# Long convolution in 64-step Toeplitz blocks on 64x64 array tiles instead of 128-step blocks on the full array

## The chip, the cores and the metric

The kernel runs on one core of a Trainium2 chip. The metric is the time of one execution in device microseconds (us). A core has TensorE (matmuls, PE in the profile, with its weight loads as PEld), VectorE (DVE), ScalarE (ACT), GpSimd (POOL), SyncE (SP, here only a queue that issues DMAs) and 16 DMA engines. SBUF is the working memory of 128 partitions, PSUM the memory that TensorE writes.

## The reference

One block of a network on `x` of shape (4, 2048, 256), all in float32: a layer norm, then the sum of a gated long convolution and a ternary feed-forward part, added to `x`. Cut to what matters:

```
xn   = layernorm(x)
proj = xn @ in_proj_w + in_proj_b              # 256 -> 768
v    = proj[..., :256]
for i in range(2):                             # the two orders
    ctrl = proj[..., (i+1)*256:(i+2)*256]
    h    = implicit_filter(...)                # (2048, 256): an MLP of time, times exp(-|decay| * t * 2048)
    v    = causal_convolution(v, h)            # along the 2048 steps, a filter of its own for each channel
    xc   = conv3(ctrl) ; v = v * xc * sigmoid(xc @ gate_w + gate_b)
attn = v @ out_proj_w + out_proj_b
r    = relu(bitlinear(xn, w_fc) + gate * low_rank(xn))        # 256 -> 1024
ffn  = bitlinear(r * r, w_proj)                               # 1024 -> 256
out  = x + attn + ffn
```

The filter decays so fast that most of its lags are below the least normal float32. The kernel measures that at run time: it always computes the lags below 257, those from 257 to 384 only for groups of channels in which one filter still has a normal number there, and all the rest only if a flag is set (with these inputs it is not).

## The kernel before, in words

Four stages follow one another, each a block in which the engines run their own programs and meet at semaphores.

**Setup** (`setup_stage`) computes the filters and writes them to `filters` in HBM, one row of 2048 + 127 values for each of 2 x 256 channels, makes the effective feed-forward weights and the flags.

**Projection** (`project_stage`) runs over 16 chunks of 512 tokens, software-pipelined in `step`. For each chunk TensorE makes the control channels `pc` (24 matmuls of 512 columns), then `pn` = V (24 matmuls of 256 columns), then the gates of the chunk before (`gates(0)`, `gates(1)`, 24 of 512), and between them the transposes of the next chunk (`pT`, 8) and of the first gate (`pn`, 8). A product of two float32 operands is made here of three matmuls in the type fp32r, high by high, high by low and low by high (`split_mm`), for which ScalarE makes `xn_hi` as a copy and VectorE `xn_lo` as a difference. V is stored as `V[128, 256 channels, 4 batches, 16 blocks]`: time step within a block of 128 on the partitions.

**Mix** (`mix_stage`) runs over 64 groups of 8 channels (32 groups for each order, GPI = 4 groups to an iteration `it`, 16 iterations), and interleaves the convolution with the feed-forward part of one chunk for each iteration. With blocks of 128 steps the convolution of a channel is a sum over block lags A: output block a gets `T_A` (a 128x128 Toeplitz matrix of the filter) times input block a - A. `conv` issues for each channel and each of A = 0, 1, 2 one plain float32 matmul with `T_A` as the weights and the 4 x (16 - A) block columns of V as the moving side. The Toeplitz matrices are read from `filters` by DMA with overlapping rows (`hankel`): each of the four loads of a group brings two channels of 128 x 384 values into one of four slots of `T`, and waits for the matmuls that read the slot (`tile_mm`). `near(q)` is the pair of channels q. On TensorE a group reads: near(0), the middle block lag if the group's flag is set (`Tmid`, only the pairs whose bit is set), fc(2g), near(1), proj(2g-1), fc(2g+1), near(2), near(3), proj(2g). `fc` is 6 matmuls of 512 columns into `pf`, `proj` 8 matmuls of 256 columns into `pp`, both fp32r. From `pf` the value goes ScalarE relu (`r`), VectorE square, ScalarE `r_hi`, VectorE `r_lo`, and `proj` waits for that (`r_split`). VectorE moves a finished group from `py` to V (`V<-py`), multiplied with GC1 in the first order.

**Output** (`output_stage`) transposes V, multiplies by the second gate, projects and adds, in 16 chunks.

SP's queue issues the loads of `T` and `Tmid` in program order, with a wait before each. POOL's queue issues the chunk loads `xm`, `xb` and stores `xf`. TensorE runs its program in order. What a float32 matmul is on this chip shows in the trace: each plain float32 matmul leaves two LDWEIGHTS and two MATMUL records of the same shape, each fp32r matmul and each transpose one of each.

Of the kernel before, what the change touches and what calls it, by code (L numbers as in the profile page):

```python
# [23 lines left out]
COLS = B * NA  # L24
PADDED = P - 1 + L
NEAR = 3
MID_FROM = (NEAR - 1) * P + 1
FAR_FROM = NEAR * P + 1
FARS = (NA - NEAR - 1) // NEAR
GC = 8  # L30
TC = 2
TILES = GC // TC
# [10 lines left out]
def setup_stage(nc, hbm, ident, bv_row, srow, flag, V, GC1, Win, Wgate, eps, half, load_first, norm):  # L43
    (in_w, in_b, out_b, freqs, w1, b1, w2, b2, w3, b3, decay, gate_w, fast_b, w_fc, w_proj, u, v, gate,
     filters, fc_hi, fc_lo, proj_t) = hbm
    with ExitStack() as ctx:
# [36 lines left out]
        zpad = sb("zpad", [P, 4, P - 1])  # L83
        ones = sb("ones", [P, P])
        win_f = sb("win_f", [P, KT, 3 * D])
# [16 lines left out]
        tile_reach = sb("tile_reach", [1, GROUPS, TILES])  # L102
# [5 lines left out]
        FREQ_LOADS, RANK_LOADS, FILTER_LOADS, PROJ_LOADS, TERN_LOADS = 4, 4, 11, 3, 2  # L108
# [9 lines left out]
        peak_ready, peakT_mm = sem("peak_ready"), sem("peakT_mm")  # L118
# [7 lines left out]
        def _(sp):  # L126
# [27 lines left out]
            load(win_f[:, :, :], in_w.rearrange("(k p) c -> p k c", p=P), proj_in)  # L154
            load(gw_f[:, :, :], gate_w.rearrange("o (k p) c -> p (o k) c", p=P), proj_in)
            load(bv_row[:, :], bass.AP(in_b.tensor, 0, [[0, P], [1, D]]), proj_in)
# [4 lines left out]
            load(rows[:, KT:2 * KT, 0:P - 1], zpad[:, KT:2 * KT, :], stored)  # L161
            for w in range(4):
                sp.wait_ge(h_ready, w + 1)
                at = 0 if w < KT else P - 1
                load(filters[w * P:(w + 1) * P, at:at + L], hT[:, w, :], stored)
# [6 lines left out]
            sp.wait_ge(stored, 16 * 9)  # L172
# [17 lines left out]
        def _(dve):  # L190
# [92 lines left out]
            dve.tensor_copy(srow[:, :], ps[:, 4, 0:D])  # L283
# [3 lines left out]
            link(dve.tensor_reduce(tile_reach[:, :, :], ps[0:1, 5, :].rearrange("p (g q c) -> p g q c", q=TILES, c=TC), AX.X, ALU.max))  # L287
            link(dve.tensor_scalar(reach[:, 0:1], reach[:, 0:1], LEAST_NORMAL, None, ALU.is_ge))
            link(dve.tensor_scalar(tile_reach[:, :, :], tile_reach[:, :, :], LEAST_NORMAL, None, ALU.is_ge))

            groups = reach[:, 1:1 + GROUPS]
            link(dve.tensor_scalar(groups, tile_reach[:, :, TILES - 1], 2.0, None, ALU.mult))
            for q in range(TILES - 2, -1, -1):
                link(dve.tensor_tensor(groups, groups, tile_reach[:, :, q], ALU.add))
                if q:
                    link(dve.tensor_scalar(groups, groups, 2.0, None, ALU.mult))
# [153 lines left out]
def project_stage(nc, x, xnT_hbm, gc2_hbm, ident, bv_row, V, GC1, Win, Wgate, eps, xt, x_loaded, xn_ready, norm, taps, bias_in, gc2_saved):  # L450
    with ExitStack() as ctx:
# [7 lines left out]
        xn = [sb("xn_hi", [P, KT, CH], F32R), sb("xn_lo", [P, KT, CH], F32R)]  # L459
        ctrl = [sb(f"ctrl{i}", [P, 4, CH + 2]) for i in range(2)]  # L460
# [3 lines left out]
        xc = sb("xc", [P, 4, CH])  # L464
        kw, cb, kb, gb = taps[:, :, 0:3], taps[:, :, 3], taps[:, :, 4], taps[:, :, 5]
        pT = ctx.enter_context(nc.psum_tensor("pT", [P, KT, CH], F32))
        pn = ctx.enter_context(nc.psum_tensor("pn", [P, TT, D], F32))
# [4 lines left out]
        xn_hi_done, xn_split = sem("xn_hi_done"), sem("xn_split")  # L472
# [34 lines left out]

        def tapped(buffer, c, k):

            at = 2 - k if c < KT else k  # L510
            return buffer[:, c, at:at + CH]
# [42 lines left out]
        def _(dve):  # L554
# [4 lines left out]
            def step(s, s0):  # L559
# [19 lines left out]
                def tap(c, k_, before, done):  # L579
                    if back:  # L580
                        dve.wait_ge(before, 4 * s - 4 + c + 1)
                        dve.scalar_tensor_tensor(out=xc[:, c, :], in0=tapped(ctrl[1 - par], c, k_), scalar=kw[:, c, k_:k_ + 1],  # L582
                                                 in1=xc[:, c, :], op0=ALU.mult, op1=ALU.add).then_inc(done, 1)

                def low(c):
                    if back:
                        dve.wait_ge(xc_hi_done, 4 * s - 4 + c + 1)
                        dve.tensor_tensor(xcs[c // KT][1][:, c % KT, :], xc[:, c, :], xcs[c // KT][0][:, c % KT, :].bitcast(F32),  # L588
                                          ALU.subtract).then_inc(xc_split, 1)

                def gated(c):
                    dve.wait_ge(gate_done, 4 * s - 4 + c + 1)
                    dve.tensor_tensor(xc[:, c, :], pc[:, c, :], xc[:, c, :], ALU.mult).then_inc(gc_done, 1)
# [19 lines left out]
                if front:  # L613
                    dve.wait_ge(v_mm, s + 1)
                    dve.tensor_tensor(V[:, :, bass.ds(batch(dve, s, s0), 1), TT * k:TT * k + TT].rearrange("p c n a -> p c (n a)"),
                                      pn[:, :, :].rearrange("p i c -> p c i"),
                                      bv_row[:, :].unsqueeze(2).broadcast_to([P, D, TT]), ALU.add).then_inc(v_stored, 1)
# [3 lines left out]
                if ahead:  # L621
                    dve.wait_ge(xn_hi_done, s + 2)
                    if s0 >= 0:
                        dve.wait_ge(xn_saved[1], 16 * s + 16)
                    dve.tensor_tensor(xn[1][:, :, :], pT[:, :, :], xn[0][:, :, :].bitcast(F32), ALU.subtract).then_inc(xn_split, 1)  # L625
# [8 lines left out]
        def _(act):  # L634
# [4 lines left out]
            def step(s, s0):  # L639
# [9 lines left out]
                def first_tap(c):  # L649

                    if back:
                        act.wait_ge(halo_done, 4 * s + c + 1)
                        act.activation(xc[:, c, :], tapped(ctrl[1 - par], c, 0), ACT.Identity, bias=kb[:, c:c + 1],  # L653
                                       scale=kw[:, c, 0:1]).then_inc(tap0_done, 1)

                def high(c):
                    if back:
                        act.wait_ge(xc_ready, 4 * s + c + 1)
                        act.activation(xcs[c // KT][0][:, c % KT, :], xc[:, c, :], ACT.Copy).then_inc(xc_hi_done, 1)
# [661 lines left out]
```

## Time and profile before

| | us |
|---|---|
| median of 3 runs | 1172.76 |
| lowest and highest | 1154.29, 1172.95 |
| the profiled execution, its own time | 1176.48 |
| its span, first to last instruction | 1174.8 |
| mean granted TensorE clock | 0.949 of full speed |

The span and the profiled execution's own time differ by 1.7 us, which lie around the instructions. By stage the span divides into setup 0 to 72, projection 72 to 361, a gap up to 379, mix 379 to 1080, a gap up to 1102, output to the end. In the rows below a time is in us from the span's start unless marked ns; a row of the timeline has start, duration, engine, line, operation, output and inputs and, in brackets, the engine's idle time before it and what ended it. A matmul's duration runs from its start to its modelled end, so that the durations of neighbours overlap; the distance between starts is the pace.

### The profile page before, as it was taken

The numbers are of one execution on the slowest core, as the hardware profiler recorded it, in microseconds if no ns is written. First come the engines' busy times: TensorE is split into PE (matmuls) and PEld (weight loads), VectorE is DVE, ScalarE is ACT, GpSimd is POOL, SyncE is SP. The second block draws the span as 40 slices with busy tenths as digits, with TensorE's granted clock in tenths as the row PEclk, the third lists the DMA queues.
The fourth block names the chain that finished last, engine by engine and source line by source line (L and its number), as shares of the span: only waits on it lengthen the run. The fifth ranks groups of instructions, "written<-read, shape, count | busy, mean of one in ns | idle before, by whom it ended". The sixth has DMA issues, their size and how long they took to land. (4 is left out here: it accounts for less than half of the span.)

```text
span 1174.8 us, 21456 instructions
## 1 busy us (share of the span) xinstructions
PE 1056.6 (90%) x6948; PEld 942.7 (80%) x6949; DVE 624.5 (53%) x1031; ACT 434.6 (37%) x598; POOL 235.2 (20%) x267
## 2 busy tenths in 40 slices
PE   6768999999973999999999999999999999997597
PEld 3357788877863989889898898898898999997586
DVE  7848999999982333333343342342343443343486
ACT  5326777777771222222221122122222222221573
POOL 1044556545601001101101101100101101100011
PEclk9869999999996999989998899998999999999799
DMA  6253323332316888887886897977977877888297
GB/s 168 114 197 127 127 94 138 143 125 92 124 72 218 191 221 191 201 224 147 207 206 158 207 217 192 237 183 164 232 204 176 226 192 189 215 189 266 80 373 266
DMA packets 123605, 214.09 MB, mean 182 GB/s; under 512 B 14212, under 2 KB 101268, under 8 KB 122292
## 3 DMA queue, kind: packets, MB, share of 16 engines
q1 hardware_dynamic: 111572, 168.46, 56.0%
q0 software_dynamic: 11568, 42.08, 9.8%
q10 hardware_dynamic: 432, 3.15, 0.7%
q8 instruction: 17, 0.28, 0.1%
q14 instruction: 16, 0.13, 0.0%
HBM read 164.11 MB, written 49.54 MB: 182 GB/s over the span
## 5 line engine op out<-in xcount | busy, mean ns | idle before, releaser
L999 PEld LDWEIGHTS py<-V,T 128*128 128x128 f32 x3072 | 375.9, 195 | 48.8 <-issue 38.3
L999 PE MATMUL py<-V,T 128*128 x3072 | 373.5, 275 | 30.7 <-DMA T<-filters 30.3
L923 DVE TENSOR_TENSOR r<-r 128x512 f32<-128x512 f32 x128 | 88.6, 692 | 345.3 <-ACT r L951 345.3
L951 ACT ACTIVATE r<-pf 128x512 f32<-128x512 f32 x128 | 76.5, 597 | 461.5 <-PE pf L400 450.4
L925 DVE TENSOR_TENSOR r_lo<-r,r_hi 128x512 fp32r<-128x512 f32 x128 | 92.6, 724 | 89.2 <-ACT r_hi L954 89.2
L984 PE MATMUL pp<-wproj,r_hi 128*128 128x256 f32 x512 | 139.1, 305 | 0.0
L984 PE MATMUL pp<-wproj,r_lo 128*128 128x256 f32 x512 | 129.6, 286 | 0.0
L954 ACT ACTIVATE r_hi<-r 128x512 fp32r<-128x512 f32 x128 | 80.8, 631 | 97.1 <-DVE r L923 97.1
L398 PE MATMUL pf<-xm_hi,wfc_hi 128*128 x256 | 111.9, 437 | 0.7 <-DMA xm_hi<-xnT_hbm 0.5
L582 DVE SCALAR_TENSOR_TENSOR xc<-ctrl,taps,xc 128x512 f32<-128x512 f32 x128 | 99.8, 799 | 17.3 <-ACT xc L653 16.1
L439 POOL TENSOR_SCALAR xt<-xt,norms 128x256 f32<-128x256 f32 x64 | 107.2, 1687 | 3.4 <-POOL norms L433 3.4
L399 PE MATMUL pf<-xm_hi,wfc_lo 128*128 x256 | 103.9, 406 | 0.0
L400 PE MATMUL pf<-xm_lo,wfc_hi 128*128 x256 | 103.8, 406 | 0.0
L984 PEld LDWEIGHTS pp<-wproj,r_lo 128*128 128x128 f32 x512 | 99.9, 195 | 0.0
L984 PEld LDWEIGHTS pp<-wproj,r_hi 128*128 128x128 f32 x512 | 99.3, 194 | 0.0
L872 POOL DMA_DIRECT2D xm_hi<-xnT_hbm x16 | 9.3, 580 | 320.1 <-PE pf L400 250.6
L398 PE MATMUL pc<-xc_hi,wgate_hi 128*128 128x512 f32 x128 | 54.2, 423 | 18.8 <-DVE xc_lo L588 18.8
L879 POOL TENSOR_TENSOR xb<-xb,bo_row 128x1024 f32<-128x1024 f32 x16 | 37.9, 2371 | 148.7 <-DMA xb<-in_attn_x 148.7
L400 PEld LDWEIGHTS pf<-xm_lo,wfc_hi 128*128 128x128 f32 x256 | 50.3, 196 | 12.1
L398 PE MATMUL pc<-xn_hi,win_hi 128*128 128x512 f32 x128 | 53.6, 419 | 4.9 <-DVE xn_lo L625 4.9
L398 PEld LDWEIGHTS pf<-xm_hi,wfc_hi 128*128 128x128 f32 x256 | 50.7, 198 | 7.4 <-issue 1.0
L653 ACT ACTIVATE xc<-ctrl,taps 128x512 f32<-128x512 f32 x64 | 51.9, 810 | 11.1 <-DVE ctrl L576 8.5
(163 smaller groups left out, 1646.6 us busy)
## 6 DMA issues: line engine op xcount, KB each, us to landing
T<-filters SPq DMA_DIRECT2D x256, 384.0 KB, 6.3
xt<-in_attn_x SPq DMA_DIRECT2D x16, 512.0 KB, 4.1
xnT_hbm<-xn_hi SPq DMA_DIRECT2D x16, 512.0 KB, 4.3
xnT_hbm<-xn_lo SPq DMA_DIRECT2D x16, 512.0 KB, 3.8
gc_hbm<-xc SPq DMA_DIRECT2D x16, 512.0 KB, 2.6
xm_hi<-xnT_hbm POOLq DMA_DIRECT2D x16, 512.0 KB, 5.4
xm_lo<-xnT_hbm POOLq DMA_DIRECT2D x16, 512.0 KB, 8.1
xb<-in_attn_x POOLq DMA_DIRECT2D x16, 512.0 KB, 9.6
```

What stands on the lines that cost most here:

```text
L398: pe.matmul(out, w[0], x[0], start=start, stop=False, **more)
L399: pe.matmul(out, w[1], x[0], start=False, stop=False, **more)
L400: return pe.matmul(out, w[0], x[1], start=False, stop=stop, **more)
L439: last = pool.tensor_scalar(buf[:, i, :], buf[:, i, :], mv[:, i, 0:1], rs[:, i:i + 1], ALU.subtract, ALU.mult)
L582: dve.scalar_tensor_tensor(out=xc[:, c, :], in0=tapped(ctrl[1 - par], c, k_), scalar=kw[:, c, k_:k_ + 1], in1=xc[:, c, :], op0=ALU.mult, o ...
L653: act.activation(xc[:, c, :], tapped(ctrl[1 - par], c, 0), ACT.Identity, bias=kb[:, c:c + 1], scale=kw[:, c, 0:1]).then_inc(tap0_done, 1)
L923: dve.tensor_tensor(r[j][:, :], r[j][:, :], r[j][:, :], ALU.mult).then_inc(sq_done, 1)
L925: dve.tensor_tensor(r_lo[j][:, :], r[j][:, :], r_hi[j][:, :].bitcast(F32), ALU.subtract).then_inc(r_split, 1)
L951: act.activation(r[j][:, :], pf[j][:, :], ACT.Relu).then_inc(relu_done, 1)
L954: act.activation(r_hi[j][:, :], r[j][:, :], ACT.Copy).then_inc(r_hi_done, 1)
L984: last = pe.matmul(pp[:, i, :], part[m % 2][:, i * P:(i + 1) * P], wproj[:, m, :], start=(m == 0 and n == 0 and i % 2 == 0), stop=(m == HT ...
L999: last = pe.matmul(y[:, c, :, A:NA], tile[:, j * P:(j + 1) * P], V[:, bass.ds(m * (GPI * GC) + (g * GC + c), 1), :, 0:NA - A] .rearrange(" ...
```

## The change: blocks of 64, four tiles, V as one float32 product

The block is now BW = 64 steps, and a time step within a block takes 64 partitions. The other partition half holds other channels: V is `[128, 128 slots, 4, 32 blocks]`, where a channel lives on partition half `side` and in one of 128 slots. A group is again 8 channels: PAIR = 2 values l, two halves q of the slots, two partition halves `side`. `conv` issues for each l and each A = 0..4 (NEAR is 5) four float32 matmuls with 64x64 weights and 4 x (32 - A) moving columns, one for each pair (side, q): rows of the array by `side`, columns and output partitions by `q`, output bank by `side`. Their moving side is `vwin`, a copy of the group's part of V that ScalarE makes one group ahead. The filters are stored in another order of rows, so that a group's loads are two DMAs of 64 partitions x 4 channels x 320 values, into one of two buffers `T0`, `T1`, which are free when the group two before is done (`group_mm`). The middle lags are now two blocks of 64 (MID = 2) for all 8 channels of a flagged group, loaded into one of two `Tmid`. On TensorE a group reads: conv of l = 0, the middle if flagged, fc(2g), proj(2g-1), fc(2g+1), conv of l = 1, proj(2g).

In the projection, V is one plain float32 product: weights `xnT` (128 x 64 tokens), moving side the 128 columns of one half of the channels, output on partitions 0 to 63 or 64 to 127, 32 matmuls a chunk. For it ScalarE copies `pT` to `xnT` ahead of `xn_hi`, and VectorE takes `xn_lo` from `xnT`. The transposes, the stores of the gates and their loads in the output stage follow the new layout, in the same count of TensorE instructions; the second gate's load is two DMAs of 64 partitions. Setup stores the filters in more DMAs (the second order's rows by halves), stores the 256 scales to HBM, from where the mix stage reads them back, and has a shorter chain of flag instructions.

The core of the diff ("..." marks what is left out):

```diff
-NEAR = 3
+BW = 64
+SIDES = P // BW
+SLOTS_V = D // SIDES
+TB = CH // BW
+NB = L // BW
+NEAR = 5
+MID = 2
 GC = 8
-TC = 2
-TILES = GC // TC
+PAIR = GC // SIDES // SIDES
...
@@ projection, ScalarE, ahead of xn_hi @@
                     if s0 >= 0:
+                        act.wait_ge(v_mm, s + 1)
+                        act.wait_ge(xn_split, s + 1)
+                    act.activation(xnT[:, :, :], pT[:, :, :], ACT.Copy).then_inc(xnT_done, 1)
+                    if s0 >= 0:
                         act.wait_ge(xn_saved[0], 16 * s + 16)
                     act.activation(xn[0][:, :, :], pT[:, :, :], ACT.Copy).then_inc(xn_hi_done, 1)
...
@@ projection, TensorE @@
-                    for i in range(TT):
-                        ts = slice(i * P, (i + 1) * P)
+                    pe.wait_ge(xnT_done, s + 1)
+                    for i in range(TB):
+                        ts = slice(i * BW, (i + 1) * BW)
                         for k in range(KT):
-                            last = split_mm(pe, pn[:, i, :], (xn[0][:, k, ts], xn[1][:, k, ts]),
-                                            (Win[0][:, k, 0:D], Win[1][:, k, 0:D]), k == 0, k == KT - 1)
+                            for side in range(SIDES):
+                                last = pe.matmul(pn[side * BW:(side + 1) * BW, i, :].rearrange("p (h c) -> p h c", h=KT),
+                                                 xnT[:, k, ts], Wv_sides[:, k, :, side, :], start=(k == 0), stop=(k == KT - 1))
...
@@ mix, SP @@
+                        def load(buf, A0, count, s):
+                            first = lags(order, A0, count)
+                            for side in range(SIDES):
+                                row = channels(m, g) * SIDES + (order * D + side * SLOTS_V)
+                                sp.dma_start(buf[side * BW:(side + 1) * BW], hankel[:, bass.ds(row, SIDES * PAIR), first:first + count * BW]).then_inc(s, 16)
+
+                        wait_alone(sp, group_mm, G + 1, sp_passed)
+                        load(T[g % 2], 0, NEAR, T_loaded[g % 2])
+                        middle = sp.value_load(flag[0:1, bass.ds(G + 1, 1)], min_val=0, max_val=1)
                         with sp.If(middle > 0):
...
+                            load(Tmid[g % 2], NEAR, MID, mid_loaded[g % 2])
...
@@ mix, ScalarE @@
+            def window(order, m, it, g):
+                G = it * GPI + g
+                act.wait_ge(group_mm, G + 1)
+                if order:
+                    act.wait_ge(y_out, G - GROUPS // ORDERS + 3)
+                act.activation(vwin[g % 2][:, :, :, :, :].rearrange("p b l n a -> p b l (n a)"),
+                               Vs[:, :, bass.ds(channels(m, g), PAIR), :], ACT.Copy).then_inc(window_done, 1)
...
@@ mix, TensorE @@
                             for A in range(A0, A0 + count):
                                 j = A - A0 if order else A0 + count - 1 - A
-                                last = pe.matmul(y[:, c, :, A:NA], tile[:, j * P:(j + 1) * P],
-                                                 V[:, bass.ds(m * (GPI * GC) + (g * GC + c), 1), :, 0:NA - A]
...
+                                for side in range(SIDES):
+                                    rows = slice(side * BW, (side + 1) * BW)
+                                    for q in range(SIDES):
+                                        last = pe.matmul(py[g % 2][q * BW:(q + 1) * BW, side, l, :, A:NB],
+                                                         tile[rows, q * PAIR + l, j * BW:(j + 1) * BW],
+                                                         vwin[g % 2][rows, q, l, :, 0:NB - A],
+                                                         start=(l == 0 and A == 0), stop=True, skip_group_check=True)
...
                         pe.wait_ge(y_out, G + 1)
-                        near(0)
+                        pe.wait_ge(window_done, G + 1)
+                        wait_alone(pe, T_loaded[g % 2], it * (GPI * 8 * SIDES) + (g // 2 + 1) * (16 * SIDES), pe_passed)
+                        conv(T[g % 2], 0, 0, NEAR)
...
                         fc(it, 2 * g, m % 2)
-                        near(1)
                         if g > 0:
                             proj(it, 2 * g - 1)
                         fc(it, 2 * g + 1, m % 2)
-                        near(2)
-                        near(3)
+                        conv(T[g % 2], 1, 0, NEAR).then_inc(group_mm, 1)
                         proj(it, 2 * g)
```

TensorE in the mix stage, between the second `fc` and the `proj` that ends a group. A row is line, operation, output and inputs, output partitions by columns, and what it waits for; before:

```order
L400 MATMUL pf<-xm_lo,wfc_hi 128x512
L999 MATMUL py<-V,T 128x64 [waits T_loaded2]
L999 MATMUL py<-V,T 128x4x15
L999 MATMUL py<-V,T 128x4x14
L999 MATMUL py<-V,T 128x64
L999 MATMUL py<-V,T 128x4x15
```

and now:

```order
L413 MATMUL pf<-xm_lo,wfc_hi 128x512
L1064 MATMUL py<-vwin,T 64x128 x4
L1064 MATMUL py<-vwin,T 64x4x31 x4
L1064 MATMUL py<-vwin,T 64x4x30 x4
L1064 MATMUL py<-vwin,T 64x4x29 x4
L1064 MATMUL py<-vwin,T 64x4x28 x4
```

Twelve matmuls in two waiting pieces (the six rows' pattern comes twice) become twenty in one piece without a wait, each on a 64x64 tile, four to a block lag.

ScalarE in the projection, around the copies of the transposed tokens; before:

```order
L663 ACTIVATE pc<-pc,taps 128x512 [waits gate_mm] x2
L689 REGISTER_ALU
L691 REGISTER_ALU [waits xT_mm]
L692 ACTIVATE xn_hi<-pT 128x1024 [waits xn_hi_saved]
L663 ACTIVATE pc<-pc,taps 128x512 [waits gate_mm] x2
```

and now:

```order
L687 ACTIVATE pc<-pc,taps 128x512 [waits gate_mm] x2
L713 REGISTER_ALU
L715 REGISTER_ALU [waits xT_mm]
L717 ACTIVATE xnT<-pT 128x1024 [waits xn_split,v_mm]
L719 REGISTER_ALU
L720 ACTIVATE xn_hi<-pT 128x1024 [waits xn_hi_saved]
L687 ACTIVATE pc<-pc,taps 128x512 [waits gate_mm] x2
```

One more copy of 1024 values a partition stands ahead of `xn_hi` and of the last two sigmoids.

## Rows read from the trace of the kernel before

**Rows 1.** The page: busy times of the engines over the span.

```profile
span 1174.8 us, 21456 instructions
PE 1056.6 (90%) x6948; PEld 942.7 (80%) x6949; DVE 624.5 (53%) x1031; ACT 434.6 (37%) x598; POOL 235.2 (20%) x267
```

**Rows 2.** Stretches by stage: busy time and count of each engine, clock, DMA.

```profile
core 0: us, PE busy (x) PEld busy (x) DVE busy (x) ACT busy (x) POOL busy (x), PEclk, DMA share, GB/s
...
72.10:361.30 289.20, 264.32 (x1408) 221.73 (x1408) 246.88 (x536) 199.99 (x290) 135.60 (x150) 0.96 0.30 111
...
379.00:1080.00 701.00, 678.27 (x4912) 634.17 (x4912) 260.29 (x351) 157.23 (x256) 73.83 (x76) 0.97 0.82 200
```

**Rows 3.** Groups of instructions: busy us, mean ns, idle time before them.

```profile
L999 PEld LDWEIGHTS py<-V,T 128*128 128x128 f32 x3072 | 375.9, 195 | 48.8 <-issue 38.3
L999 PE MATMUL py<-V,T 128*128 x3072 | 373.5, 275 | 30.7 <-DMA T<-filters 30.3
...
L999 PE MATMUL py<-V,Tmid 128*128 x48 | 8.4, 304 | 9.7 <-issue 8.1 <-DMA Tmid<-filters 1.5
```

**Rows 4.** Timeline of TensorE, one whole group in the mix stage.

```profile
451.36 2.78 PE L999 MATMUL py<-V,T 128*128 x24
453.96 0.37 PE L984 MATMUL pp<-wproj,r_hi 128*128 128x256 f32 x1
...
455.00 1.44 PE L999 MATMUL py<-V,T 128*128 x12
456.25 0.47 PE L398 MATMUL pf<-xm_hi,wfc_hi 128*128 x1
...
457.72 1.44 PE L999 MATMUL py<-V,T 128*128 x12
458.98 0.36 PE L984 MATMUL pp<-wproj,r_hi 128*128 128x256 f32 x1
...
461.40 2.78 PE L999 MATMUL py<-V,T 128*128 x24
```

**Rows 5.** Waits in the mix stage: total us, times, longest us.

```profile
PE py L999 <- DMA T<-filters: 30.3, 21, 18.6
...
PE py L999 <- issue: 8.1, 6, 2.5
```

**Rows 6.** Projection, float32 transposes of 128 moving columns: their group, and the timeline.

```profile
L749 PE MATMUL pT<-ident,xt 128*128 128x128 f32 x128 | 17.5, 282 | 5.2 <-PEq L46 5.2
...
290.80 1.03 PE L749 MATMUL pT<-ident,xt 128*128 128x128 f32 x8
291.59 0.48 PE L398 MATMUL pc<-xc_hi,wgate_hi 128*128 128x512 f32 x1
```

**Rows 7.** Timeline around V's product, the first and the last of its 24 records.

```profile
284.02 0.28 PE L398 MATMUL pn<-win_hi,xn_hi 128*128 128x256 f32 x1
...
286.74 0.28 PE L400 MATMUL pn<-win_lo,xn_hi 128*128 128x256 f32 x1
287.89 0.49 PE L398 MATMUL pc<-xc_hi,wgate_hi 128*128 128x512 f32 x1 [0.87 <-DVE xc_lo L588]
```

**Rows 8.** Timeline of a step's end in the projection, on three engines.

```profile
291.95 1.03 ACT L692 ACTIVATE xn_hi<-pT 128x1024 fp32r<-128x1024 f32 x1 [0.26 <-PE pT L749]
...
292.34 1.28 DVE L593 TENSOR_TENSOR xc<-pc,xc 128x512 f32<-128x512 f32 x2
...
293.54 1.21 DVE L625 TENSOR_TENSOR xn_lo<-pT,xn_hi 128x1024 fp32r<-128x1024 f32 x1
295.28 0.48 PE L398 MATMUL pc<-xn_hi,win_hi 128*128 128x512 f32 x1
```

**Rows 9.** DMA issues: KB each, median us from issue to landing.

```profile
T<-filters SPq DMA_DIRECT2D x256, 384.0 KB, 6.3
...
Tmid<-filters SPq DMA_DIRECT2D x11, 512.0 KB, 6.1
```

**Rows 10.** Timeline from the last fc of an iteration to its proj.

```profile
1075.11 2.78 PE L999 MATMUL py<-V,T 128*128 x24
1075.38 0.60 ACT L951 ACTIVATE r<-pf 128x512 f32<-128x512 f32 x1 [1.69 <-PE pf L400]
...
1077.40 0.69 DVE L925 TENSOR_TENSOR r_lo<-r,r_hi 128x512 fp32r<-128x512 f32 x1 [0.69 <-ACT r_hi L954]
1077.70 0.37 PE L984 MATMUL pp<-wproj,r_hi 128*128 128x256 f32 x1
```

More of the change, by code:

```diff
@@ L817, in lags, with channels @@
         def lags(order, A0, count):
-            return P * (NA - A0 - count) if order == 0 else P * A0
+            return BW * (NB - A0 - count) if order == 0 else BW * A0
+        def channels(m, g):
+            return m * (GPI * PAIR) + g * PAIR
         @block.sync
         def _(sp):
-            sp.sem_inc(tile_mm, TILES)
-            sp.sem_inc(mid_loaded, 16)
+            sp.sem_inc(group_mm, 2)
+            for i in range(2):
+                sp.sem_inc(mid_loaded[i], 16 * SIDES)
             tail = sp.value_load(flag[0:1, 0:1], min_val=0, max_val=1)
@@ L830, in body @@
                         G = it * GPI + g
-                        row = m * (GPI * GC) + (order * D + g * GC)
-                        def load(slot, q, A0, s):
-                            first = lags(order, A0, NEAR)
-                            sp.dma_start(T[:, slot, :, :], hankel[:, bass.ds(row + q * TC, TC), first:first + NEAR * P]).then_inc(s, 16)
-                        wait_alone(sp, tile_mm, G * TILES + 1, sp_passed)
-                        load(0, 0, 0, T_loaded[0])
-                        wait_alone(sp, tile_mm, G * TILES + 2, sp_passed)
@@ L854, in loads @@
+                            sp.sem_inc(mid_loaded[g % 2], 16 * SIDES)
+                        if far:
+                            wait_alone(sp, group_mm, G + 2, sp_passed)
+                            for j in range(FARS):
+                                load(T[1 - g % 2], NEAR + MID + NEAR * j, NEAR, far_loaded)
+                                wait_alone(sp, far_used, G * FARS + (j + 1), sp_passed)
                 groups(sp, order, body)
@@ L1014, in body @@
                         with pe.If(middle > 0):
[L1015 to L1023 removed]
+                            wait_alone(pe, mid_loaded[g % 2], it * (GPI * 8 * SIDES) + (g // 2 + 2) * (16 * SIDES), pe_passed)
@@ L1024, in body @@
+                            for l in range(PAIR):
+                                conv(Tmid[g % 2], l, NEAR, MID)
+                        for j in range(FARS if far else 0):
+                            wait_alone(pe, far_loaded, G * (16 * SIDES * FARS) + 16 * SIDES * (j + 1), pe_passed)
+                            for l in range(PAIR):
+                                last = conv(T[1 - g % 2], l, NEAR + MID + NEAR * j, NEAR)
                             last.then_inc(far_used, 1)
                         fc(it, 2 * g, m % 2)
-                        near(1)
@@ L1050, in sem @@
             return ctx.enter_context(nc.semaphore(name))
[L1052 removed]
+        ys = [sb(f"ys{i}", [P, TB, SLOTS_V]) for i in range(2)]
         yg = [sb(f"yg{i}", [P, KT, CH]) for i in range(2)]
```

256 lines of the change are left out of this document (134 added, 122 removed).

## Prediction

> **What bounds the kernel now.** I read the page's first part for the shares [rows 1], then the stretches by stage [rows 2]. TensorE is busy 678 of 701 us in the mix stage and 264 of 289 us in the projection, more than any other engine in both; these two stages are 990 of 1175 us. A modelled busy time doesn't tell what a record costs, so the paces come from the timeline. In one group of the mix stage [rows 4] the 24 records of the convolution from 451.36 take until 453.96, 2.60 us; the 12 from 455.00 take 1.25 and the 12 from 457.72 take 1.26 us. A group has 48 such records (8 channels x 3 lags x 2), and they take 5.11 us, **106.5 ns each**, of a group's 10.04 us (451.36 to 461.40). Is that pace set by the weights or by the columns? The transposes of the projection [rows 6] are float32 with 128 moving columns: eight of them last 1.03 us together and one alone 0.282, so (1.03 - 0.28)/7 = 107 ns lie from start to start, which is 0.84 ns a column. The convolution's records have 64, 60 or 56 columns, so their columns need 47 to 54 ns. The pace of 106.5 ns is then that of loading 128 columns of weights, 0.83 ns a column, and the moving side is hidden under it. Beside this the mix stage waits 11.7 us for T after its first load (30.3 less the first, 18.6) [rows 5].
>
> **The convolution's records.** Per group the change makes 2 values l x 5 lags x 4 tiles = 40 matmuls, 80 records, for 48. Their weights have 64 columns: 80 x 0.83 x 64 = 4.26 us if weight loads follow one another at the pace of today. Their moving sides have 4 x (32 - A) = 128 to 112 columns, 120 on average, 0.84 x 120 = 101 ns a record. 80 of them in a row are 8.06 us. So all depends on whether matmuls on different tiles run side by side, which no row shows; the bounds are 8.06 us (never) and 2.0 us (always four). TensorE takes matmuls in order, and the two records of one float32 matmul use the same tile, one after the other. The second record of one tile can then run beside the first of the next tile, and no more than that: one slot of 101 ns for each of 40 matmuls, 4.03 us. The larger of 4.26 (weights) and 4.03 (columns) is my value, as tiles that hold different rows or columns of the array share nothing that the program names: **4.26 for 5.11 us, -0.85 x 64 groups = -54 us**.
>
> **The middle lags.** Before, 48 records in 11 loads [rows 3, 9], 5 us. The normal numbers between lags 257 and 384 lie in 12 channels by the reference's own inputs, which fall into 12 groups in the new order. Each takes 2 x 2 x 4 = 16 matmuls, 32 records, 384 in all, at 53 ns 20.5 us: **+15 us**. The wait ahead of them for the branch, 8.1 us in 6 cases [rows 5], stays.
>
> **The loads of T.** 1024 rows of 1536 bytes a group (four loads of 384 KB [rows 9]) become 512 rows of 1280 bytes, 0.42 of the bytes, and a load has a whole group of about 9 us to land, where the median was 6.3 us with the DMA engines 82% busy [rows 2, 9]. So the 11.7 us of waits go: **-12 us**; the first load of the stage, 18.6 us, stays, since it hangs on the queue's start and on the stores and loads around it. SP's queue holds nothing else that is due in this stage. POOL's and the weights' transfers see a quieter memory, which nobody waits for.
>
> **ScalarE's window and VectorE's move.** The copy `vwin` of 512 values a partition costs 0.6 us, as `r_hi` does. ScalarE is busy 157 of 701 us [rows 2]; the copy waits for the end of the group before and stands ahead of the relu of fc(2g), which comes only after the first half convolution and an fc, over 3 us later. Cost 0. VectorE's move has the same 512 values. What becomes late next is `proj(it, 7)`: now its last `r_lo` ends 3.0 us after the last fc ([rows 10], 1075.11 to 1078.09), under 2.6 us of convolution and 0.95 us of proj. Afterwards the cover is 2.13 + 0.95 = 3.1 us. Nothing is left over, and if the convolution gets faster than I say, this wait takes some of it back, at most 1 us x 16.
>
> **The projection.** V's product was 24 records from 284.02 to 286.86, 2.84 us a chunk [rows 7]. It becomes 32 matmuls, 64 records with 64 weight columns (3.4 us) and 128 moving columns of 107 ns; the two column halves pair as above, 32 x 107 = 3.42 us. That is +0.6 us, but right behind it TensorE stands idle 0.87 us for `xc_lo` of the chunk before [rows 7], a chain on ScalarE and VectorE that V's product does not touch. So +0.6 us goes into the idle time; without a pairing it is 6.85 us, +4.0 less the 0.87. The new copy `xnT` takes 1.03 us like `xn_hi` [rows 8] and stands ahead of it. `xn_lo` would then start at 294.05 and end at 295.26, and the next step's first matmul starts at 295.28: it just fits. It delays two sigmoids too, which VectorE wants only after its statistics. Bounds 0 and 16 x 1.03; I take **+4 us** for the stage. Setup's and the output stage's edits (smaller flag chain, a few more DMAs, the same number of records) I cost at 0, with ±3 us.
>
> **The sum.** -54 + 15 - 12 + 4 = -47 us on the profiled execution's own 1176.5 gives 1129.5. That execution is 3.7 us above the median of the runs shown, so **1126 us**.
>
> **Rivals.** (1) *Each change of tile shape empties the array.* The tiles stand between fc and proj on the full array, four changes of shape a group, 256 in the mix stage, 32 in the projection. A change can cost nothing, or all that is hidden now: the rest of the last matmul and an uncovered weight load, 275 - 107 + 195 = 363 ns [rows 3]. At half of that, 0.18 us, the mix stage gains back 46 us and the projection 3 in what its idle time leaves: **1175 us**, with ends at 1126 and 1225. For it: no two shapes lie next to each other in a busy stretch of this trace, so nothing contradicts it. The Trainium skill, TensorEngine Tiling (Array Packing), section Key Properties, says that changing the tiling mode, not just the tile, drains TensorE; no run here shows that yet, and this rival is what it would mean.
>
> (2) *Tiles pair only where their rows of the array differ.* In the order (side, q) each second step changes only the column half. Of 8 slots in four matmuls 6 remain: 6.05 us a group, +0.94 x 64 = +60, the middle +20, the projection +50 (its halves differ in columns only, +4.0 - 0.87 = 3.1 x 16), the loads -12: **1291 us**. The Trainium skill, TensorE: Matmul & The Clock Gate, Part 3, says that a weight load overlaps a running matmul only with another row group; the trace speaks against it for the full array, where loads of 195 ns run under matmuls of 275 ns at a pace of 106.5 ns on the same rows [rows 3, 4].
>
> (3) *No pairing at all; slower than before.* A float32 matmul might hold the whole array for its two records. (8.06 - 5.11) x 64 = +189, the middle 384 x 0.84 x 106 ns = 34 us, +29, the projection +50, the loads -12: **1429 us**. The point from which it decides is 5.11 us a group, that is 128 ns for each of the 40 matmuls: above it the convolution is slower than before. For it speaks that the trace has not one matmul beside another.
>
> (4) *More than pairs.* If also weights load side by side, the columns' 4.03 us hold: -69 + 12 - 12 + 4, **1108 us**; with all four tiles at once 2.0 us, some 970 us, against the order of the two records.
>
> **Chances.** My forecast 0.37, spread over 1100 to 1150. Rival 1 0.24, (2) 0.07, (3) 0.13, (4) 0.13 with 0.03 of it far down, anything else (an operation that loads its weights slower on a tile, a clock that falls in the stage, which has 0.97 now) 0.06. The range takes in the forecast, rivals 1 and 2 and most of 4, and leaves out 3 and the far ends: 1075 to 1295. The likeliest case alone spans 1100 to 1150. The three runs of the kernel before lie 1.6% apart, so about 2%, 23 us, is what a measurement can tell from no change. Faster by more than that needs a time below 1149: the forecast, rival 4 and a little of rival 1, 0.53. Within it lies rival 1 for the most part, 0.18; slower 0.29.
>
> **What the new profile would show.** The 80 records of a group take 4.3 us between the first conv and fc and between fc and proj: 2.1 us from the start of a half convolution to the next kind of record. Starts of records on one tile 100 ns apart, the first of the next tile beside them, would confirm the pairing; even spacing of 100 ns for all of them is rival 3, of 53 ns my case with weights as the bound. Where a half convolution starts or ends, a step over 0.2 us is rival 1. Waits of `py` for T after the first should be under 2 us, the projection's step about 16.8 us, and ScalarE must show no wait of TensorE for `vwin`. The prediction is wrong by far if the clock granted in the mix stage falls because the tiles count as less work, or if `proj` starts to wait for `r_lo` in every group.

## The result, and the profile after

The changed kernel takes **1036.8 us** (median of 4 runs, 1030.3 to 1040.0), the kernel before 1171.0 in the same set: ratio 0.892, 95% interval 0.879 to 0.904. Measured again beside the experiments it is 1033.6 us (0.882, 0.878 to 0.886). The forecast was 1126 and the low end of its range 1075: the sign was right, the size was not, and the time lies below the range.

The page's first part, for [rows 1]:

```profile
span 1037.4 us, 26543 instructions
PE 891.8 (86%) x9972; PEld 725.5 (70%) x9973; DVE 624.8 (60%) x1025; ACT 478.2 (46%) x678; POOL 248.7 (24%) x268
```

The stretches of the projection and the mix stage, for [rows 2]:

```profile
72.00:365.00 293.00, 276.09 (x2034) 225.67 (x2035) 242.63 (x534) 210.03 (x303) 147.99 (x150) 0.97 0.29 110
365.00:391.00 26.00, 2.57 (x16) 1.96 (x14) 1.70 (x3) 3.50 (x5) 4.29 (x7) 0.60 0.88 258
391.00:942.00 551.00, 500.37 (x7296) 411.42 (x7296) 264.78 (x351) 188.17 (x318) 73.33 (x74) 0.99 0.64 144
```

The groups that answer to [rows 3], with the two that wait in the stage:

```profile
L1064 PE MATMUL py<-vwin,T 64*64 64x128 f32 (+4 forms) x5120 | 162.4, 268 | 31.9 <-DMA T<-filters 31.1
L1064 PEld LDWEIGHTS py<-vwin,T 64*64 64x64 f32 x5120 | 134.8, 133 | 63.9 <-issue 56.5
...
L1047 PE MATMUL pp<-wproj,r_hi 128*128 128x256 f32 x512 | 135.7, 298 | 17.4 <-DVE r_lo L964 17.4
...
L411 PE MATMUL pf<-xm_hi,wfc_hi 128*128 x256 | 108.5, 424 | 19.6 <-issue 12.1
```

There are 5120 records for 3072, and their modelled busy time fell from 373.5 to 162.4 us: records of 268 ns that overlap in time count once. The timeline of TensorE over a first half convolution, for [rows 4]:

```profile
401.94 0.28 PE L1047 MATMUL pp<-wproj,r_lo 128*128 128x256 f32 x1
402.15 1.25 PE L1064 MATMUL py<-vwin,T 64*64 64x128 f32 x40
403.70 0.50 PE L411 MATMUL pf<-xm_hi,wfc_hi 128*128 x1 [0.30 <-issue]
```

Forty records last 1.25 us to their modelled end, 31 ns each, where the forecast had 53. The same view, cut off at 402.17 and then at 402.5, counts the starts:

```profile
402.15 0.33 PE L1064 MATMUL py<-vwin,T 64*64 64x128 f32 x3
```

```profile
402.15 0.56 PE L1064 MATMUL py<-vwin,T 64*64 64x128 f32 x12
```

Three records have started within 20 ns, twelve within 0.35 us. The starts come in fours, 6 to 7 ns apart, and the fours are 95 to 109 ns apart (160 at the first): each four holds one record of each tile. All four tiles run at once, at the pace of one tile's columns.

The waits in the mix stage, for [rows 5]:

```profile
PE py L1064 <- DMA T<-filters: 31.1, 9, 23.8
PE pp L1047 <- DVE r_lo L964: 17.4, 33, 1.5
PE pf L411 <- issue: 12.1, 41, 0.7
PE pf L411 <- DMA xm_lo<-xnT_hbm: 7.4, 10, 0.8
...
PE py L1064 <- DMA Tmid<-filters: 2.2, 4, 0.9
```

And V's product, for [rows 7]:

```profile
341.13 3.71 PE L757 MATMUL pn<-win_v,xnT 128*64 128x128 f32 x64
344.77 0.50 PE L411 MATMUL pc<-xc_hi,wgate_hi 128*128 128x512 f32 x1
```

**Where the time went.** From the first matmul of the stage to the last, mix fell from 700.5 to 550.2 us, 150.3 us. I take each kind of piece by its median, from its start to the start of the next kind, and what the sum of a kind has over its count x median as stalls (the last row, the cost of the half clock, is an estimate):

| mix stage | us |
|---|---|
| convolution: 2 x 1.186 us a group for 5.11, x 64 | -175 |
| pieces of fc, proj and the middle, medians | +6 |
| ahead of fc and the middle: the flag's load, and 10 waits for `xm_lo` | +30 |
| waits of `proj` for `r_lo` | +17 |
| T waits after the first (11.7, now 7.3) | -4 |
| gaps ahead of the middle in the kernel before | -12 |
| stretches at half clock (44.5 us, now 6.1) | -15 |

Their sum is -153. Outside it the setup took 3 us more, the projection 4, the gap ahead of mix 5 (the first T wait went from 18.6 to 23.8), and what follows mix 1. -150 + 13 = -137; the spans differ by 137.4.

### The profile page after: what moved, and what is told of

The parts are those of the page before. It is cut to its first block and busy times, and to the rows that moved or that the text cites. A ratio compares the mean times of both kernels' runs of the same rounds, so it can differ in the third digit from the quotient of the medians.

```text
span 1037.4 us, 26543 instructions
## 1 busy us (share of the span) xinstructions
PE 891.8 (86%) x9972; PEld 725.5 (70%) x9973; DVE 624.8 (60%) x1025; ACT 478.2 (46%) x678; POOL 248.7 (24%) x268
## 5 line engine op out<-in xcount | busy, mean ns | idle before, releaser
L1064 PE MATMUL py<-vwin,T 64*64 64x128 f32 (+4 forms) x5120 | 162.4, 268 | 31.9 <-DMA T<-filters 31.1
L1064 PEld LDWEIGHTS py<-vwin,T 64*64 64x64 f32 x5120 | 134.8, 133 | 63.9 <-issue 56.5
L964 DVE TENSOR_TENSOR r_lo<-r,r_hi 128x512 fp32r<-128x512 f32 x128 | 100.0, 781 | 89.6 <-ACT r_hi L1000 89.6
L1047 PE MATMUL pp<-wproj,r_hi 128*128 128x256 f32 x512 | 135.7, 298 | 17.4 <-DVE r_lo L964 17.4
L411 PE MATMUL pf<-xm_hi,wfc_hi 128*128 x256 | 108.5, 424 | 19.6 <-issue 12.1
L1047 PEld LDWEIGHTS pp<-wproj,r_hi 128*128 128x128 f32 x512 | 96.4, 188 | 33.1 <-DVE r_lo L964 13.7
L452 POOL TENSOR_SCALAR xt<-xt,norms 128x256 f32<-128x256 f32 x64 | 115.5, 1814 | 3.4 <-POOL norms L446 3.4
L413 PE MATMUL pf<-xm_lo,wfc_hi 128*128 x256 | 100.6, 393 | 0.0
L757 PEld LDWEIGHTS pn<-win_v,xnT 128*64 128x64 f32 x1024 | 55.6, 137 | 5.8 <-issue 5.8
L757 PE MATMUL pn<-win_v,xnT 128*64 128x128 f32 x1024 | 59.4, 274 | 0.0
```

What stands on the lines that cost most here:

```text
L411: pe.matmul(out, w[0], x[0], start=start, stop=False, **more)
L413: return pe.matmul(out, w[0], x[1], start=False, stop=stop, **more)
L452: last = pool.tensor_scalar(buf[:, i, :], buf[:, i, :], mv[:, i, 0:1], rs[:, i:i + 1], ALU.subtract, ALU.mult)
L757: last = pe.matmul(pn[side * BW:(side + 1) * BW, i, :].rearrange("p (h c) -> p h c", h=KT), xnT[:, k, ts], Wv_sides[:, k, :, side, :], sta ...
L964: dve.tensor_tensor(r_lo[j][:, :], r[j][:, :], r_hi[j][:, :].bitcast(F32), ALU.subtract).then_inc(r_split, 1)
L1047: last = pe.matmul(pp[:, i, :], part[m % 2][:, i * P:(i + 1) * P], wproj[:, m, :], start=(m == 0 and n == 0 and i % 2 == 0), stop=(m == HT ...
```

## The experiments

Eleven variants ran, and the changed kernel once more. Where a median of a piece is given, it is from its first matmul's start to that of the next kind. The half convolution of the changed kernel is 1.186 us ahead of `proj` and 1.527 ahead of `fc`.

### Is it the order of the tiles, or are the tiles free?

First, tile by tile in place of lag by lag:

```diff
-for A in range(A0, A0 + count):
-    for side in range(SIDES):
-        for q in range(SIDES):
+for side in range(SIDES):
+    for q in range(SIDES):
+        for A in range(A0, A0 + count):
```

> The 20 matmuls of a half convolution in another order: all five lags of one tile, then all five of the next. Theory A (each tile works off its own records in order, and the others don't wait for it): a half convolution still takes about 1.2 us to the next kind of record, and the kernel stays within 1.5% of 1037 us. Theory B (records start strictly in program order, and four run abreast only because four tiles stand next to each other): 40 records of 100 ns one after another, with the last of a tile beside the first of the next, 3.8 us instead of 1.2, so +2.6 x 128 = +333 us, about 1370 us.

Measured: 1239.3 us, slower than the kernel before (ratio 1.056, 1.048 to 1.063). Each half convolution takes 3.24 us:

```profile
504.62 3.31 PE L1064 MATMUL py<-vwin,T 64*64 64x128 f32 x40
507.87 0.39 PE L1047 MATMUL pp<-wproj,r_hi 128*128 128x256 f32 x1
```

Neither expectation came true. The starts in the trace, in ns from the piece's first, say why (the first two records of a tile are known by their form, 128 columns without a gap):

```
tile 1:   0  161  269  375  481  584  686  786  886  981
tile 2: 692  852  961 1067 ...
tile 3: 1385 1545 ...
```

The second tile's first record starts at 692, right behind the first tile's seventh, while three earlier records of the first tile (786, 886, 981) have not started. A record passes earlier ones of another tile, but here not more than three.

Then three of four tiles without their lags 1 to 4, and as its opposite all lags 1 to 4 on one tile:

```diff
+if A % NEAR and (side or q):
+    continue
```

> Leaves out lags 1 to 4 (and the second middle lag) on three of the four tiles; the tile of partitions 0 to 63 and output partitions 0 to 63 keeps all five. 16 of 40 records of a half convolution remain. Theory A (four tiles abreast, a lag costs what its slowest tile costs): the half convolution stays at 1.2 us, the kernel at 1037 us within 1%. Rival (each record costs issue or weight-load time of its own, some 25 ns, and the tiles' overlap hides nothing): 16/40 of 1.0 us, -0.6 x 128 = -77 us, 960 us.

> Lags 1 to 4 of all four tiles are sent to one tile (partitions 0 to 63, output partitions 0 to 63), with the same count and shapes of matmuls; only lag 0 still uses four tiles. The output is not the convolution. If the gain is the tiles' running abreast: a half convolution has 2 + 32 slots of 100 ns and some 0.2 us of edges, 3.6 us instead of 1.2, +2.4 x 128 = +307 us, about 1345 us. If the gain is that 64 columns of weights load faster or that small records are cheap, it stays near 1037 us, or rises at most to the weight loads' pace of 53 ns, 40 x 53 = 2.1 us a half, +0.9 x 128 = +115 us, 1150 us.

Measured: with three tiles idle 1017.3 us (0.867, 0.858 to 0.875) and 1.166 us a piece for 1.186, though three tiles have 2 records left of 10: a tile costs nothing beside another. The rest is the piece ahead of `fc`, 1.166 us for 1.527 (52 of them, 19 us): with fewer records ahead of it the flag's load may begin sooner, which was not tried by itself. On one tile 1297.3 us (1.105, 1.097 to 1.113), 3.587 us a piece where 3.6 was expected:

```profile
500.90 3.66 PE L1066 MATMUL py<-vwin,T 64*64 64x128 f32 x40
504.49 0.38 PE L1047 MATMUL pp<-wproj,r_hi 128*128 128x256 f32 x1
```

Its total lies under the expected one since a long piece also hides the flag's load, `r_lo` and T: behind the first load of T, its trace has no wait in the stage.

Two tiles of the same rows abreast (loops side, A, q):

> The changed kernel with the loops of a half convolution in the order side, lag, column half: two tiles alternate (same rows of the array, other columns), then the other two. The same 20 matmuls. Theory (a record may start ahead of at most 3 earlier ones, and tiles are otherwise independent): two tiles run abreast for ten matmuls of 2 x 103 ns, twice: 10 x 0.206 = 2.06 us and the entry and exit, a half convolution of 2.2 us for 1.19, +1.0 us x 128 = +131, less 14 us of waits for r_lo that vanish: about 1150 us. Rival (tiles on the same rows of the array do not run side by side, my rival 2): 20 x 0.206 = 4.1 us, +2.9 x 128 = +375: about 1400 us. Only pairs from one record of a tile to the next (my forecast): 20 x 103 ns = 2.1 us too, so this run doesn't tell my forecast from the theory, as the given order and the tile-by-tile order do.

Measured: 1082.2 us (0.929, 0.907 to 0.951), 1.872 us a piece:

```profile
507.90 1.94 PE L1064 MATMUL py<-vwin,T 64*64 64x128 f32 x40
```

The rival of 4.1 us falls: tiles on the same rows run side by side. But the theory's 2.2 us is missed too. The third tile starts at 700 ns, right behind the seventh records of the first two (687, 694), and passes **six** earlier records, three on each. So the three are counted for each tile, not in all. A last run tells these two readings apart by blocks of two lags a tile:

```diff
+for first in range(A0, A0 + count, 2):
     for side in range(SIDES):
         for q in range(SIDES):
+            for A in range(first, min(first + 2, A0 + count)):
```

> The changed kernel with the matmuls of a half convolution in blocks of two lags for each tile: lags 0 and 1 on the first tile, then on the second, third and fourth; then lags 2 and 3 likewise, then lag 4. The same 20 matmuls. Theory after e1_tile_major and e9_two_abreast (each tile takes its own records in order and up to three may wait at it beside the one that runs; only a fourth holds up the records behind it, for whatever tile): a block gives a tile four records, one running and three waiting, so nothing is held up and all four tiles run abreast: a half convolution of 1.19 us as in the given order, and 1030 to 1040 us for the kernel. Rival (the reading before e9: a record starts ahead of at most three earlier ones of all tiles together): the second tile starts at once, the third and fourth wait, a half convolution of 1.6 to 1.9 us, +50 to +90 us, 1080 to 1125 us.

Measured: 1051.6 us (0.900, 0.893 to 0.907), 1.250 us a piece:

```profile
504.69 1.32 PE L1065 MATMUL py<-vwin,T 64*64 64x128 f32 x40
```

All four tiles start within 40 ns. The reading in all (1.6 us and more) falls, that for each tile stands. 64 ns over 1.186 were not foreseen: at the second block three tiles get their first record in time (495 to 521 ns) and their second at 641 to 668 ns, 43 ns later than the first tile's distance of 104 ns would have it. I take this for the load of that record's weights, which comes so late in program order; it was not tried. 128 x 0.064 = 8 us of the 18 over the changed kernel; a longer wait for the flag (1.705 us ahead of `fc` for 1.522) makes some 7 more.

### Does a change of tile shape cost anything?

The flag is now loaded behind the first half convolution. One load moved first; the same in the kernel before:

```diff
+middle = pe.value_load(flag[0:1, bass.ds(G + 1, 1)], min_val=0, max_val=1)
 pe.wait_ge(y_out, G + 1)
...
 conv(T[g % 2], 0, 0, NEAR)
-middle = pe.value_load(flag[0:1, bass.ds(G + 1, 1)], min_val=0, max_val=1)
```

> TensorE's sequencer reads the group's flag ahead of the first half convolution instead of behind it. Theory: the step from the first half convolution to fc (1.53 us in 52 groups, against 1.19 us from the second one to proj) has 0.34 us that the sequencer needs for the load of the flag and the branch, which 1.2 us of matmuls no longer cover. Then -0.34 x 52 = -18 us, 1019 us. Rival: the 0.34 us is the price of changing from tiles to a 512-column matmul on the full array: no change, 1037 us.

> The kernel before the change, with nothing but the flag read ahead of the first pair of channels. Theory D (the stretches at half clock in its mix stage, 44 us, which cost some 20 us, follow idle gaps of 1 to 2.7 us, mostly behind the flag's load ahead of the middle lags): gaps fall from 11 to under 4 us and half of the half-clock time goes: -15 us, 1156 us. Rival (the half-clock stretches have nothing to do with these gaps): at most the gaps' own 7 us, 1164 us, with the half-clock time as before.

Beside them the changed kernel once more:

> The changed kernel once more, as the base of this set: 1037 us.

Measured: 1019.1 us (0.868, 0.863 to 0.873), 14.5 under the changed kernel of the same set; the piece ahead of `fc` fell from 1.522 to 1.187. One such piece, where the first timeline above has an idle time of 0.30 us:

```profile
499.68 1.26 PE L1064 MATMUL py<-vwin,T 64*64 64x128 f32 x40
500.86 0.50 PE L411 MATMUL pf<-xm_hi,wfc_hi 128*128 x1
```

`proj(it, 7)` waits longer for `r_lo`: its step of 16 records grew from 2.92 to 3.26 us. In the kernel before, the earlier load brought 0.6%, at the edge of what the interval can tell (0.994, 0.989 to 1.000). Its gaps ahead of the middle stayed (a median of 1.99 us for 2.24, and 25.4 us for 25.5 in all), and so did its half clock, 45 us for 44.5. So this run does not say whether fewer gaps would bring less half clock; the last section of the experiments asks that again.

Both halves of the convolution in one piece between fc(2g+1) and proj(2g), which leaves two of four changes of shape a group, with the flag's load in the middle and first:

```diff
+fc(it, 2 * g, m % 2)
+if g > 0:
+    proj(it, 2 * g - 1)
+fc(it, 2 * g + 1, m % 2)
 conv(T[g % 2], 0, 0, NEAR)
...
-fc(it, 2 * g, m % 2)
-if g > 0:
-    proj(it, 2 * g - 1)
-fc(it, 2 * g + 1, m % 2)
 conv(T[g % 2], 1, 0, NEAR).then_inc(group_mm, 1)
```

> Both half convolutions of a group stand together between fc(2g+1) and proj(2g), the flag still between them: two changes of tile shape a group instead of four, 128 fewer. Theory C (a change from tiles to the full array and back costs about 0.17 us each, 0.35 us for a piece of tiles among full-array work): -64 x 0.35 = -22 us; the wait of proj(it, 7) for r_lo, 0.9 us x 15, falls away as well, since 2.3 us of convolution and 0.95 us of proj stand ahead of it: -14 us; the flag's 0.34 us is half covered, -10 us: about 990 us. Rival (the edges of a piece are only waits that come by chance): no more than the 14 us, 1023 us.

> As the kernel with both half convolutions in one piece, with the flag read at the start of the group. By theory C plus the flag's theory: -22 - 14 - 18 = -54 us, about 983 us. If reading the flag early costs as much as late: as the kernel before it in this set.

Measured: 987.7 us (0.842, 0.837 to 0.846) and **960.9 us** (0.819, 0.814 to 0.823), the fastest here. The second, over one piece:

```profile
499.94 2.28 PE L1064 MATMUL py<-vwin,T 64*64 64x128 f32 x80
502.15 0.39 PE L1047 MATMUL pp<-wproj,r_hi 128*128 128x256 f32 x1
...
504.57 0.49 PE L411 MATMUL pf<-xm_hi,wfc_hi 128*128 x1 [0.25 <-DMA xm_hi<-xnT_hbm]
```

80 records take 2.21 us for 2 x 1.186 = 2.37, and the fc and proj pieces of a group 4.87 us for 5.07: 0.36 us for two changes less. The waits for `r_lo` are gone too, since 2.2 us of convolution now stand between the last fc and its proj.

The opposite, one piece more, with the flag's load first: fc(2g) between the lags 0 to 2 and 3 to 4 of the first half.

```diff
-conv(T[g % 2], 0, 0, NEAR)
+conv(T[g % 2], 0, 0, NEAR, range(0, 3))
+fc(it, 2 * g, m % 2)
+conv(T[g % 2], 0, 0, NEAR, range(3, NEAR))
...
-fc(it, 2 * g, m % 2)
```

> The changed kernel with the flag load first in a group, as in e5_flag_first (1019 us), and the first half convolution cut in two: lags 0 to 2, fc(2g), lags 3 and 4, then proj(2g-1) and the rest as before. Two more changes of tile shape a group, the same matmuls. Theory (0.18 us for each change of shape, as read from two fewer in e6): 128 x 0.18 = +23 us over e5_flag_first, about 1042 us, and the two parts of the piece last 1.19 + 0.36 us less what now lies beside fc. Rival (the gain of e6 came from fewer waits for r_lo and T, not from the changes of shape): 1019 to 1025 us.

Measured: 1026.9 us (0.883, 0.868 to 0.899), 8 over e5_flag_first where 23 were expected. Its pieces, the second part of one group (x16) and the first part of another (x24):

```profile
500.26 0.62 PE L1064 MATMUL py<-vwin,T 64*64 64x116 f32 x16
500.82 0.39 PE L1047 MATMUL pp<-wproj,r_hi 128*128 128x256 f32 x1
...
506.93 0.87 PE L1064 MATMUL py<-vwin,T 64*64 64x128 f32 x24 [1.19 <-DMA T<-filters]
507.73 0.50 PE L411 MATMUL pf<-xm_hi,wfc_hi 128*128 x1
```

By the medians two more changes cost what two less had given back: 0.795 + 0.551 + 1.584 us from the first part to proj(2g-1) for 1.187 + 1.492, and 1.060 for 0.953 us for the proj piece, +0.36 us a group, **0.18 us a change**, 23 us in all. The total does not show it. By the one trace of each, other waits fell: `r_lo` 15.7 to 8.6 us, `Tmid` 6.7 to none, half clock 16.4 to 3.2 us (worth 6 to 7), against 5 us more for T. By the total alone, 8 us, the expectation's rival (up to 6) would have looked as good.

### What brought the half clock?

> The kernel before without its middle lags (the threshold of the flags is set so high that no group is ever flagged; the lags from 257 to 384 are left out of the result). The trace of the kernel before has TensorE at half clock for 45 us of the mix stage, the changed kernel for 6 us, and the half clock of before follows the middle pieces, ahead of which TensorE stands idle up to 2.7 us. If those gaps bring the half clock: it falls from 45 to at most 15 us in the mix stage, and the time by 8 us (the middle's records), 12 us (the gaps) and some 15 us (the clock), to about 1137 us. If the two only lie near each other: the half clock stays about 45 us and the time falls by the records and the gaps alone, to about 1152 us.

```diff
-tile_reach[:, :, :], LEAST_NORMAL, None, ALU.is_ge
+tile_reach[:, :, :], 1e30, None, ALU.is_ge
```

Measured: 1149.5 us (0.987, 0.970 to 1.004; the interval is too wide to decide by the time), half clock 34 us of the mix stage: by the clock neither of the two. The timeline of the kernel before around the first stretch inside its mix stage:

```profile
518.89 1.44 PE L999 MATMUL py<-V,T 128*128 x12
522.79 1.09 PE L999 MATMUL py<-V,Tmid 128*128 x4 [2.46 <-issue]
523.65 0.77 PE L398 MATMUL pf<-xm_hi,wfc_hi 128*128 x1
524.23 0.63 PE L399 MATMUL pf<-xm_hi,wfc_lo 128*128 x1
524.65 0.63 PE L400 MATMUL pf<-xm_lo,wfc_hi 128*128 x1
```

and of the one without the middle lags, near the same place:

```profile
526.89 1.44 PE L999 MATMUL py<-V,T 128*128 x12
530.59 1.75 PE L999 MATMUL py<-V,T 128*128 x7 [2.25 <-DMA T<-filters]
```

In both the granted clock is at its lower level, 1.2 GHz, from about 2.5 us after the gap's start, for 10.2 us, and a matmul of `fc` steps by 0.43 us for 0.23. A gap was followed by half clock whatever made it: with the middle gone, waits for T made gaps in other places. Over all fourteen traces of this case, behind the stage's first 12 us, each of the six gaps of 2.39 us or more between two starts was followed by 3 to 10 us at half clock, and 9 of the 39 between 1.25 us and that. The other three of the 18 stretches began 2.2 to 3.2 us behind the start of gaps of 0.87 to 1.25 us. So a gap's length alone does not settle it, and that the gaps are the cause is read from this order in time and from the kernels of the next sentence, which differ from the kernel before in more than their gaps. The kernels whose pieces leave no gap over 1.5 us (e1, e3, e4, e6) have none after the stage's first 12 us. In the changed kernel's two traces the longest are 1.8 and 2.2 us, with no half clock behind them.

## Why the prediction was wrong, step by step

- **The bound of the convolution** [rows 3, 4, 6] was read rightly: 106.5 ns by weights before, and today one tile's record steps by 95 to 109 ns, its columns (101 forecast).
- **The step that failed** is "The second record of one tile can then run beside the first of the next tile, and no more than that", with "TensorE takes matmuls in order" ahead of it: the overlap of the tiles. The runs e1, e9 and e11 show instead that a tile takes its own records in order while up to three more wait at it, and records of the other tiles go past. In the given order the tiles fill evenly, so none is held up by another and all four run at once. -175 us for -54. The outcome was in the text as "all four tiles at once 2.0 us, some 970 us", with 0.03.
- **The weights**: 80 x 0.83 x 64 = 4.26 us would have been a floor if loads followed one another. They do not: 80 records start in 2.0 us, so loads of 133 ns on different tiles overlap as well (5120 of them have a busy time of 134.8 us), and e9 shows it for tiles on the same rows. The Trainium skill, TensorE: Matmul & The Clock Gate, Part 3, says that a load overlaps only with another row group, the rule that I weighed in rival 2; it doesn't hold here. The Trainium skill, TensorEngine Tiling (Array Packing), Key Properties, says that tiles load and multiply independently; the 6 to 7 ns between their starts agree.
- **Rival 1 was true too.** 0.18 us for each change of shape in e6 and in e10, its middle value, which was half of a bound and no reading, so that it came out so near is luck; 256 x 0.18 = 46 us are what the changed kernel pays in the mix stage. I had set it against the forecast as a case of its own; it was a term to be added. The Trainium skill, TensorEngine Tiling (Array Packing), Key Properties, says that changing the mode drains TensorE and gives no price; 0.18 us is the price here. With four abreast and this cost the sum would have been: 2.0 us of records a group instead of 4.26 is -145, +46 for the changes, 1126 - 99 = 1027. That this is within 10 us of the result is partly chance: the convolution and its changes brought 169 us (the first two rows of the table) for this sum's 153, and the terms that the sum lacks or has wrong took about as much back.
- **Rivals 2 and 3** fell: e9 has 1.87 us for two tiles on the same rows, and e3 shows what no pairing would be, 3.587 us a piece.
- **The middle**: 32 records in 0.887 us, 10.6 us in all for 20.5 forecast; before it took 8.0 us and not the 5 of the forecast, so +3 for +15. That the wait ahead of them for the branch "stays" was wrong: `near` to `mid` took 25.5 us in 11 cases, 12 more than the records, and now 1.59 us each. e7 shows that the flag's load was not its cause; that it was the four branches and `Tmid` issued only one group ahead is argued from the code and the trace, not tried.
- **T waits**: 11.7 to 7.3, -4 for -12. A group without waits is 7.4 us and not 9, so a load of 6.1 us has less cover; the bytes fell as said (DMA share 0.82 to 0.64).
- **`r_lo`**: "at most 1 us x 16" if the convolution gets faster: 17.4 us. The mechanism was right and the size near, but half of it is elsewhere: 16 waits ahead of `proj(it, 7)` are 8.7 us, and 16 ahead of `proj(it, 0)`, which has only fc(1) and a half convolution as cover, 7.2 us. It should have been in the sum of every faster case. `vwin` cost nothing, as said: no wait of TensorE for it is in the trace.
- **Not seen**: TensorE's own load of the flag behind the first half convolution. I looked at what the matmuls wait for and not at what its sequencer must do between two pieces; +0.34 us ahead of `fc` or the middle, e5 gives 14.5 us back. Nor the half clock, -15 us, though the stage "which has 0.97 now" stood in the text [rows 2]: I read it as no loss and named only a further fall.
- **The projection**: V's product 3.64 us for 3.42, which needs the two column halves abreast, as said; the idle time behind it shrank from 18.8 to 7.4 us, the wait for `xn_lo` grew by 2, and the stage grew by 4.1, forecast 4, which was a choice between the bounds 0 and 16. **Setup and output**: +3 and +1, inside ±3. The gap ahead of mix, +5, was taken as unchanged.

## What to carry to other kernels

Matmuls on small tiles of the array are worth what their columns cost divided by the tiles at work, if the program deals them out to all tiles in turn, so that no tile gets a fourth waiting record while another has nothing to do. A short run for each tile is not enough: in e9 no tile gets more than two in a row, and its piece took 1.872 us for 1.186, since two tiles filled up while the others stood idle. Put the matmuls in few long pieces, since each change to or from the full array costs 0.18 us, and put a register load where longer work stands ahead of it. When a price is set against a forecast as a rival, ask whether both can hold at once, and add them.

## What the runs showed of the hardware

- Float32 matmuls on four 64x64 tiles start 6 to 7 ns apart and run at once, two records each, 95 to 109 ns a record of 112 to 128 columns; weights of one tile load beside matmuls of the others, on the same rows too (e9).
- At a tile three records wait beside the running one; the fourth holds up the program behind it (starts at 692 ns in e1, at 700 in e9, all at once in e11).
- A change between a 64x64 tile and the full array: 0.18 us, from e6 and e10.
- A flag's load and branch on TensorE's sequencer behind a piece of 1.19 us shows as 0.30 to 0.34 us of idle time [the first timeline above].
- Behind the mix stage's first 12 us, a gap of 2.39 us or more between two starts on TensorE was followed by half clock, for 3 to 10 us, in all six cases; of 39 gaps from 1.25 us on below that, 9 were.
